# A two-layer macaron network on one core: tokens routed into a region per expert, group by group, and fp4 weights prepared inside the expert stage

## The reference

```
x = x + 0.5 * moe(norm(x))        # block 1
x = x + attention(norm(x))        # block 2, causal softmax, 16 heads
x = x + 0.5 * moe(norm(x))        # block 3, the same weights as block 1
x = x + 0.5 * fp4_ffn(norm(x))    # block 4
x = x + linear_attention(norm(x)) # block 5
x = x + 0.5 * fp4_ffn(norm(x))    # block 6, the same weights as block 4

moe(x):  e = argmax(x @ W_router)               # 4 experts, one per token
         h = gelu(x @ W1[e] + b1[e])            # 256 -> 1024
         return layer_norm(h @ Wo + bo + x) * gamma + beta
fp4_ffn: weights 704 x 256, 704 x 256 and 256 x 704, and the activations,
         quantised to fp4 and back in blocks of 16: scale = max|block| / 6,
         each value rounded to the grid 0, 0.5, 1, 1.5, 2, 3, 4, 6 times scale
```

## Time and profile before

| what | us |
|---|---|
| median of 3 runs (2399.11 to 2403.15) | 2401.53 |
| the profiled execution, time | 2399.69 |
| its span in the trace | 2397.8 |
| setup, up to the first routing stage | 17.3 |
| first routing stage: tiles, then the rest | 68.7, then 55.9 |
| first expert stage begins | 141.9 |
| second routing stage begins | 1062.4 |
| its tiles, then the rest | 73.4, then 64.9 |
| second expert stage begins | 1200.7 |
| busy over the span: TensorE, VectorE, ScalarE, GpSimd | 2047.2, 1446.0, 996.3, 970.0 |

### The profile page before, as it was taken

One profiled execution on the slowest core, in us unless ns is written; L12 is line 12 of the kernel. 1 busy time (PEld: TensorE's weight loads), 2 busy tenths in 40 slices (PEclk: granted clock), 3 DMA queues, 4 the chain that ended last, 5 costly groups with the idle time before them and its releaser, 6 DMA issues. The chain is left out here.

```text
span 2397.8 us, 43209 instructions
## 1 busy us (share of the span) xinstructions
PE 2047.2 (85%) x13577; PEld 1400.5 (58%) x13577; DVE 1446.0 (60%) x3844; ACT 996.3 (42%) x2303; POOL 970.0 (40%) x1249
## 2 busy tenths in 40 slices
PE   4359998696999999988289995899988999789996
PEld 3259897352444444437189994566665666456674
DVE  4313223667888888826623333889857676488883
ACT  1023332241666666653133332333325666534332
POOL 4422223750111111124612224666546666455652
PEclk9999999796999999999589997999999999999999
DMA  5145554346333344210255553000000000000002
GB/s 189 39 158 195 192 193 136 118 146 97 54 55 54 54 54 54 28 38 1 70 188 192 195 192 125 22 13 18 0 1 2 2 2 2 1 1 0 0 0 70
DMA packets 105499, 177.02 MB, mean 74 GB/s; under 512 B 14576, under 2 KB 70160, under 8 KB 105360
## 3 DMA queue, kind: packets, MB, share of 16 engines
q1 hardware_dynamic: 99216, 158.47, 24.0%
q0 software_dynamic: 6144, 16.79, 2.2%
HBM read 136.01 MB, written 38.93 MB: 73 GB/s over the span
## 5 line engine op out<-in xcount | busy, mean ns | idle before, releaser
L1024 DVE TENSOR_REDUCE a_part_max<-a_psS 128x1 f32<-128x512 f32 (+3 forms) x608 | 362.8, 655 | 76.2 <-PE a_psS L952 67.6
L1080 ACT ACTIVATE a_PT<-a_psE 128x512 f32<-128x512 f32 (+1 forms) x608 | 309.3, 583 | 189.1 <-PE a_psE L966 174.1
L518 PE MATMUL e_psH<-e_xsT,e_w 128*128 128x128 f32 x2240 | 266.7, 278 | 0.0
L518 PEld LDWEIGHTS e_psH<-e_xsT,e_w 128*128 128x128 f32 x2240 | 259.9, 194 | 0.6
L946 PE MATMUL a_psS<-a_sk,a_sq 96*128 96x512 bf16 (+3 forms) x768 | 234.3, 341 | 23.5 <-DMA a_sk<-qk_parts 19.6
L527 PE MATMUL e_psY<-wo_moe,e_gT 128*128 128x256 f32 x1120 | 253.0, 379 | 0.0
L927 POOL TENSOR_SCALAR_AFFINE_SELECT a_PT<-a_PT 128x512 f32<-128x512 f32 x128 | 81.5, 637 | 419.1 <-ACT a_PT L1080 419.1
L966 PE MATMUL a_psE<-a_sq,a_sk 98*128 98x512 bf16 (+3 forms) x768 | 224.6, 329 | 2.5 <-ACT a_PT L1080 1.4
L527 PEld LDWEIGHTS e_psY<-wo_moe,e_gT 128*128 128x128 f32 x1120 | 207.6, 190 | 25.4
L547 ACT ACTIVATE e_gT<-e_psH,e_bias 128x128 f32<-128x128 f32 x560 | 159.9, 369 | 138.6 <-PE e_psH L518 138.6
L567 DVE TENSOR_TENSOR e_y<-e_psY,e_xr 128x256 f32<-128x256 f32 x70 | 29.7, 425 | 308.1 <-PE e_psY L527 303.9
(11 more groups left out here) (269 smaller groups left out, 3869.1 us busy)
## 6 DMA issues: line engine op xcount, KB each, us to landing
e_w<-w_in SPq DMA_DIRECT2D x70, 1024.0 KB, 4.9
a_sq<-qk_parts SPq DMA_DIRECT2D x96, 128.0 KB, 4.4
a_sk<-qk_parts SPq DMA_DIRECT2D x96, 128.0 KB, 7.2
e_xs<-sorted_x SPq DMA_DIRECT2D x70, 128.0 KB, 2.1
e_xr<-sorted_x SPq DMA_DIRECT2D x70, 128.0 KB, 4.6
sorted_y<-e_yo SPq DMA_DIRECT2D x70, 128.0 KB
sorted_x<-zeros SPq DMA_DIRECT2D x1, 4480.0 KB, 18.8
X<-x_in SPq DMA_DIRECT2D x4, 1024.0 KB, 9.7
```

What stands on the lines that cost most here:

```text
L518: mm = pe.matmul(psH[p][:, n * P:(n + 1) * P], w1[p][:, k, n * P:(n + 1) * P], xsT[p][:, k, :], start=k == 0, stop=k == KD - 1)
L1024: dve.tensor_reduce(part_max[:, c, h0:h0 + heads, qt], psS[place % RING][:, 0:heads * n].rearrange("p (h k) -> p h k", h=heads), AX.X, ALU ...
L1080: act.activation(PT[kt % 2][:, h0:h0 + heads, q0:q0 + n], psE[e % RING][:, 0:heads * n].rearrange("p (h q) -> p h q", h=heads), ACT.Exp, s ...
```

## The change

1. **Regions.** Each expert has a region of 4224 rows in `sorted_x`, so a token's row is known from its rank within its expert, before the totals are. `choose` finds the expert for a group of four tiles, `count_up` ranks them with five matmuls, `put` makes the rows, and GpSimd scatters the group while later tiles are routed. At the end four more scatters write zeros behind each expert's last token. Tables say for each of the 35 tiles its expert and its row (`row_of`), and for each token its row in `sorted_y` (`result_row`), which stays dense.
2. **Normalisation** moves to ScalarE, straight into `XN`; the GpSimd copy goes. GpSimd takes one power for two tiles.
3. **Setup** keeps the first piece of x and the router's weights; the other loads are issued by SyncE in the first routing stage, x in pieces of four tiles.
4. **fp4 weights** are loaded in the second routing stage as before, but quantised in the second expert stage, in 18 pieces of 128 x 256, one per tile.
5. The hardware loops of routing and expert stages are written out (`loop=False`). Two constants that nothing used are dropped.

```diff
 TensorE, routing
-  [(1, project), (0, turn_y)] + [(5, router), (4, turn)]
+  [(1, project), (0, turn_y)] + [(J + 9, count_up, 4), (J + 4, router), (J + 3, turn)]    # J = 3 after attention, else 0
+            def count_up(t, p):
+                g = t // G
+                pe.wait_ge(choice, CHOICE * (g + 1))
...
+                mm = pe.matmul(psN[:, 0:GE], st.upper[:], oh[:].rearrange("p j e -> p (j e)"), start=True, stop=False,
+                               skip_group_check=True)
+                for j in range(G - 1):
+                    mm = pe.matmul(psN[:, (j + 1) * EXPERTS:GE].rearrange("p (j e) -> p j e", e=EXPERTS), st.ones[:],
...
+                if g > 0:
+                    mm = pe.matmul(psN[:, 0:GE].rearrange("p (j e) -> p j e", e=EXPERTS), st.ones[:],
...
+                mm.then_inc(ranked, 1)
 VectorE, routing
+            def choose(t, p):        # 7 chained instructions on 128 x 16
...
+            def put(t, p):           # 4 chained instructions on 128 x 16
...
+            pipeline(dve, TILES, ([(2, join)] if after_attention else []) +
+                     [(J, measure, 2), (J + 2, take_shift, 2), (J + 8, choose, 4), (J + 10, put, 4)], unroll=4, loop=False)
 ScalarE, routing
+            def norm(t, p):
+                i = p // 2
+                act.wait_ge(shifted, t // 2 + 1)
+                for j in (0, 1):
+                    act.activation(XN[:, t + j, :], st.X[:, t + j, :], ACT.Identity,
+                                   bias=shift[i][:, j:j + 1], scale=rstd[i][:, j:j + 1]).then_inc(normed, 1)
 GpSimd, routing
+            def scatter(t, p):
+                pool.wait_ge(placed, PLACED * (t // G + 1))
+                for j in range(G):
+                    pool.indirect_dma_start(st.sorted_x[:, :], bass.IndirectOffsetOnAxis(ap=st.slot[:, t + j:t + j + 1], axis=0),
+                                            XN[:, t + j, :], None).then_inc(scattered, 16)
+            pipeline(pool, TILES, [(J, root, 2), (J + 10, scatter, 4)], unroll=4, loop=False)
+            pool.wait_ge(padded, 2)
+            for e in range(EXPERTS):
+                pool.indirect_dma_start(st.sorted_x[:, :], bass.IndirectOffsetOnAxis(ap=pad_slot[:, e:e + 1], axis=0),
+                                        st.zeros[:], None).then_inc(scattered, 16)
 expert stage
+        def piece_of(t):
+            return t - 1 if fp4 and 1 <= t <= len(fp4.pieces) else None
-                sp.dma_start(xs[p][:], st.sorted_x[bass.ds(t * P, P), :]).then_inc(x_in[p], 16)
+                sp.dma_start(xs[p][:], st.sorted_x[bass.ds(row(sp, t), P), :]).then_inc(x_in[p], 16)
             def turn(t, p):                                                     # TensorE
                 pe.wait_ge(x_in[p], 8 * (t - p) + 16)
                 reuse(pe, evacuated, t)
+                if fp4:
+                    if piece_of(t - 2) is not None:
+                        pe.wait_ge(fp4.out, KD * (t - 2))
+                    if piece_of(t) is not None:
+                        fp4.turn(pe, piece_of(t), psT[p])
                 for k in range(KD):
                     mm = pe.transpose(psT[p][:, k * P:(k + 1) * P], xs[p][:, k * P:(k + 1) * P], st.ident[:])
-            pipeline(dve, SLOTS, [(0, take_bias), (2, finish), (3, norm)])
+            pipeline(dve, SLOTS, [(0, take_bias), (2, finish), (3, norm)] + ([(0, quantize_weights)] if fp4 else []),
+                     loop=False)
 class Fp4Weights
+    def turn(self, pe, n, ps):
+        pe.wait_ge(self.quant, self.STEPS * (n + 1))
+        src = self.source(n)
+        for k in range(KD):
+            mm = pe.transpose(ps[:, D + k * P:D + (k + 1) * P], src[:, k * P:(k + 1) * P], self.st.ident[:])
+        mm.then_inc(self.turned, 1)
```

More of the change, by code:

```diff
@@ L150, in _ @@
             x = st.x_in.rearrange("(t p) d -> p t d", p=P)
+            sp.dma_start(st.X[:, 0:4, :], x[:, 0:4, :]).then_inc(st.x_loaded[0], 16)
             sp.dma_start(st.w_router[:], st.router_in.rearrange("(k p) e -> p k e", p=P)).then_inc(st.router_loaded, 16)
[L152 to L161, removed]
         @block.gpsimd
@@ L279, in measure, with take_shift @@
                 take_moments_of_pair(dve, c, st.X, t, stats[i], moments[i], LN_EPS)
                 c.end()
-            def norm(t, p):
+            def take_shift(t, p):
                 i = p // 2
                 dve.wait_ge(rooted, t + 2)
[L285 to L289, removed]
@@ L310, in _ @@
[L310 to L317, removed]
@@ L342, in _ @@
[L342 to L345 removed]
+                if t >= 4:
+                    dve.wait_ge(normed, t - 2)
+                dve.scalar_tensor_tensor(out=shift[i][:], in0=moments[i][:, :, 0], scalar=-1.0, in1=rstd[i][:],
+                                         op0=ALU.mult, op1=ALU.mult).then_inc(shifted, 1)
@@ new lines, in _ @@
+            q.link(dve.scalar_tensor_tensor(out=rowf[:], in0=st.slot_f[:], scalar=float(P), in1=jump[:, 0, :],
+                                            op0=ALU.mult, op1=ALU.add))
+            for e in range(2, EXPERTS + 1):
+                if e < EXPERTS:
+                    q.done(dve.scalar_tensor_tensor(out=whichf[:], in0=st.slot_f[:], scalar=first[:, e:e + 1],
+                                                    in1=whichf[:], op0=ALU.is_ge, op1=ALU.add))
+                q.link(dve.tensor_tensor(rowf[:], rowf[:], jump[:, e - 1, :], ALU.add))
@@ L428, in _ @@
             if not after_attention:
                 pe.wait_ge(st.router_loaded, 16)
-            pipeline(pe, TILES, ([(1, project), (0, turn_y)] if after_attention else []) + [(5, router), (4, turn)],
-                     unroll=4, loop=not after_attention)
-            pe.wait_ge(sorting, 9)
-            oh = onehot[:].rearrange("p e t -> p (e t)")
-            pe.matmul(psN[:, 0:ET], st.upper[:], oh, start=True, stop=True)
-            pe.matmul(psN[:, ET:2 * ET], st.ones[:], oh, start=True, stop=True).then_inc(counted, 1)
@@ L437, in _ @@
-            if after_attention:
-                fp4.tensor(pe)
-            else:
+            pipeline(pe, TILES, ([(1, project), (0, turn_y)] if after_attention else []) +
+                     [(J + 9, count_up, 4), (J + 4, router), (J + 3, turn)], unroll=4, loop=False)
+            pe.wait_ge(placed, PLACED * NG)
+            pe.matmul(psN[:, GE:GE + EXPERTS], st.ones[:], before[NG % 2][:], start=True, stop=True).then_inc(counted, 1)
+            if not after_attention:
                 pe.wait_ge(st.weights_loaded, 16 * WEIGHT_LOADS)
@@ L529, in down_proj @@
                 mm.then_inc(down, 1)
-            pipeline(pe, SLOTS, [(0, turn), (1, up_proj), (2, down_proj)])
+            pipeline(pe, SLOTS, [(0, turn), (1, up_proj), (2, down_proj)], loop=False)
         @block.scalar
@@ L539, in evacuate @@
                                ACT.Copy).then_inc(evacuated, 1)
+                if fp4 and piece_of(t) is not None:
+                    fp4.put(act, piece_of(t), psT[p])
             def activate(t, p):
@@ L548, in activate @@
                 ins.then_inc(gelu, 1)
[L550 removed]
+            pipeline(act, SLOTS, [(0, evacuate), (1, activate)], loop=False)
         @block.vector
@@ L594, in scale @@
                 c.end()
-            pipeline(pool, SLOTS, [(0, root), (1, scale)])
+            pipeline(pool, SLOTS, [(0, root), (1, scale)], loop=False)
 class Gather:
@@ new lines, in clear, with quantize @@
+        dve.wait_ge(self.cleared, 1)
+        dve.wait_ge(self.loaded, 16 * 5)
+    def quantize(self, dve, n):
+        if n == 0:
+            self.clear(dve)
+        c = Chain(dve, self.quant, self.STEPS).at(n)
+        dve.wait_ge(self.quant, self.STEPS * n)
+        blocked = lambda a: a.rearrange("p (b e) -> p b e", e=BLOCK)
+        x, vv, mm = blocked(self.source(n)), blocked(self.v[:]), blocked(self.m[:])
+        back = quantize(dve, c, x, vv, mm, self.scale[:], self.inverse[:])
+        c.link(dve.tensor_tensor(vv, vv, mm, ALU.subtract))
+        c.done(dve.tensor_tensor(x, vv, back, ALU.mult))
+        c.end()
@@ L1918, in build @@
         st.w_down = sb("w_down", [P, KF, D])
-        run(route_phase, "r1_", True)
-        run(expert_phase, "e1_")
+        with ExitStack() as raw:
+            st.fp4 = Fp4Weights(nc, st, raw)
+            run(route_phase, "r1_", True)
+            run(expert_phase, "e1_", st.fp4)
         st.lin_w = sb("lin_w", [P, KD, 3 * D])
```

379 lines of the change are left out of this document (199 added, 180 removed).

## The result

The changed kernel takes 2455.68 us (median of 4 runs, 2454.3 to 2460.63); the kernel before, run beside it, takes 2400.34 (4 runs). The ratio is 1.0232 with a 95% interval of 1.022 to 1.0244: 2.3% slower. The forecast was 2488 with a range of 2440 to 2530. The profiled execution has a span of 2454.3 against 2397.8, so 56.5 us are to be placed.

What follows compares the result with a forecast made beforehand. TensorE was taken to bound the expert stage, a tile chain and GpSimd-only scatter tails the routing stages. 2399.7 - 35.6 (first routing) + 5 (first expert) - 30.2 (second routing) + 149 (second expert) = 2488 us; range 2440 to 2530.

Steps and rivals of the forecast that it cites:

- The stall in the second expert stage: Second expert stage: TensorE waits for each lap's quantize; 16 laps of 16.55 us against 7.49, +149 us with small terms.
- quantize hides: Rival, second expert stage: quantize runs in VectorE's idle time ahead of finish, routing gains stand; 2347 us, chance 0.06.
- The clock: Second expert stage: each pause drops TensorE to half clock for about 4 us, costing 2.0 us a lap (bounds 0 and 3).
- full clock: Rival, second expert stage: stalls as forecast, but TensorE's clock stays up; 2456 us, chance 0.16.
- Clock down all through: Rival, second expert stage: each of 16 stalled laps at half clock, costing 7.25 and not 2.0; 2572 us, chance 0.07.
- Start of routing: First routing stage: SyncE issues two small loads, so the setup barrier falls at about 5.8 instead of 17.3, -11.5 us.
- count_up: Routing stages: new TensorE matmuls cost 1.5 us a group, +10.5 in the first stage; +10 in the second.
- The tails: Both routing stages: last router to next stage shrinks to 20.7 us; -35.2 in the first, -44.2 in the second.
- routing gains halved: Rival, routing stages: GpSimd backlog and late X pieces cost +33; 2521 us, chance 0.07.
- exclusive lock: Routing scatters: if the port lock shared by VectorE and GpSimd made all issues 2.13 us long, the sum would be 2501.
- The register read: Expert stages: SyncE reads a register before token loads, 0.7 us each; +5 in the first, +3 in the second.
- The rest: Attention and the fp4 layers, outside routing and expert stages: not touched by the change, 0.

Runs made afterwards that it cites:

- x1: Changed kernel with VectorE doing the quantize first in its step instead of last: 2322.67 us, ratio 0.9676.
- x2: Changed kernel with VectorE's order kept, but TensorE takes each fp4 piece one lap later: 2322.83 us, ratio 0.9678.
- x5: Changed kernel with 48 unread identity transposes on TensorE ahead of each wait for a piece, from turn(3) on: 2421.59 us, ratio 1.0089.
- x8: Changed kernel with 2 instead of 5 matmuls in count_up, VectorE adding up the one-hot rows within the group first: 2439.6 us, ratio 1.0167.
- x6: Kernel before with the loops of both expert stages written out, nothing else: 2388.29 us, ratio 0.9956.
- x7: Changed kernel with the edits of x1 and x8 together: 2305.61 us, ratio 0.9608.
- x3: Changed kernel with the fp4 weights back at the end of the second routing stage, as before: 2353.7 us, ratio 0.9806.

## Why the prediction was right

The mechanism was the predicted one, at its predicted place, and the time lies 32 us under the forecast. That is inside the range, but below the 2465 to 2515 given for the mechanism alone.

- **The stall in the second expert stage** (+149, measured +134.3). The condition "It decides if quantize(s) ends before down(s-2) does" was put to the test by x1 and x2, and each took out 133 us, all of the slowdown and more. That is *quantize hides* made true, at 2323 where 2347 was given; 18.7 of the 24 us between them are the routing stages and the first expert stage, which came out better than forecast here too. There are 16 stalled laps and two free pieces, as counted. A lap was priced at 16.55; it takes 15.95. The term that was mis-sized is the idle: 7.0 assumed, 6.53 measured, within the bounds of 6.1 to 7.5. That is 7.5 us over 16 laps. I had let six VectorE instructions wait for GpSimd to end, from L1171 on. L1171 did not: it ran beside GpSimd and took 0.54, against 0.42 in the first stalled lap (1143.02), where GpSimd was idle. L1172 may have waited: it took 0.70 instead of 0.29, and ended 0.15 or 0.16 us behind GpSimd's L652 in each of the 15 laps behind that one. One instruction (0.42 and a gap of 0.04) is what the 7.0 had too much. Of the other 7, no run separates the parts: a lap of x5 less its wait, 13.76 less 6.45, is 7.31, where I had counted 7.25 and 0.3 (4 us over 16 laps), and the free laps gained from the written-out loops, for which I had counted nothing.
- **The clock** (2.0 a lap): 2.1 by x5 on the mean. The "about 4 us after work began" of the forecast came from one pause; here it was 2.9, 4.8 or 5.8, and that their mean of 4.5 lies so near is partly luck. This is what tells *full clock* from the forecast. That rival's number, 2456, is the measured time to the microsecond, and its mechanism is still wrong. With the clock up the changed kernel would have taken 2421.6. The two numbers meet because the routing stages gained 10.4 us more, the first expert stage 8.3 more and the second lost 14.7 less than forecast. A total alone can't confirm a mechanism. The Trainium skill (TensorE: Matmul & The Clock Gate, "HAM oscillation — how this bites in real kernels") describes such a loop, whose waits are for transfers; here the same comes from a wait for another engine, at 6.53 us of pause and 2.1 us of loss on the mean.
- ***Clock down all through*** fell: from 1183.70 on the lap runs at 1.00, and no lap looked at stays at 0.50 for more than 5.8 us of its work.
- **Start of routing** (-11.5): -12.5. First routing begins at 4.85, not 17.3.
- **count_up** (1.5 a group): 1.25, the 3.26 less 2.01 above. In the second routing stage I added 10 for it and 4 for two more steps of the pipeline. Its tiles grew from 73.4 to 80.7, by 7.3 in all, so half of that 14 was not there. x8 confirms the kind and the size.
- **The tails** (20.7 each): 21.1 in the first stage, 20.9 in the second, whose last router matmul ends at 1099.63. The scatters spread over the tiles as foreseen, and *routing gains halved* fell: 64 scatters took 0.98 us each on the mean, the longest seen 1.22, so GpSimd never fell behind. The sum by an exclusive lock did not come. The 2501 given for it holds the 13 us of one routing stage only; for both it would have been 2514. The Trainium skill (SBUF — State Buffer, "Who interferes with whom") says that a VectorE instruction with two inputs in SBUF contends with a GpSimd instruction that reads SBUF. The trace agrees in the expert stage, where L1171 took 0.54, and L1253, of the same shape and alone, 0.42. For L1171 those 0.12 us are far less than a whole GpSimd instruction (L652, 0.79). For L1172, by its 0.41 us and its end just behind L652, a wait for the whole of it is not ruled out.
- **The register read** (+5 in the first expert stage): the step's own size was right, 4.6 us by the comparison with x6. The sign of the stage came out wrong (-3.3) because I had valued the written-out loops at a mere bound, "which is in the bound 0", and x6 shows them at 7.7 and 6.3 us a stage from first load to 35th (7.0 and 5.9 over the whole stages).
- **The rest** (+2.4, forecast 0): between the first transpose of the first fp4 layer and the last store, where the code is the same, seven of the profiled kernels (all but x2, x5 and x7) took 881.4 to 884.3 us. The changed kernel took 883.3 and the kernel before 881.7, so 1.6 of it is within what these kernels differ by where their code is the same. What the remaining 0.8 is stays open.

## What to carry to other kernels

Work that another engine will wait for doesn't belong at the end of a step behind an instruction that waits for that same engine. Put it first in the step, or let the consumer ask a lap later; either was worth 5% here and cost little: from the first token load to the 35th the second expert stage takes 248.7 us in x1, against 246.3 in x3, which has no quantize in it. Ask of every added instruction what stands ahead of it in its engine's order, and not whether the engine has time. And price a regular pause of TensorE at more than its length: here 6.5 us of waiting cost 2.1 more on the mean.

## What the runs showed of the hardware that was not expected

- The same pause does not cost the same each time. Behind a constant 6.53 us TensorE ran at 1.2 GHz for about 2.9, 4.8 or 5.8 us, in turn, and lost 1.3, 2.2 or 2.7 us by it (the changed kernel's laps of 15.2, 16.1 and 16.6 us less x5's 13.77 and the 0.08 by which x5 waits less).
- The clock column of a view can say 1.00 where rows show 1.2 GHz: the router's four loads took 0.93 us throughout the first routing stage, as at 0.50 in the second.
- The expert stages' hardware loops cost 14.0 us between the first and the 35th token load of the two stages (x6, 249.7 to 242.0 and 248.4 to 242.2), though TensorE was nearly full there; 9.9 of it reached the kernel's time.
- One read of a register from a table ahead of a load moves that load by 0.72 us on SyncE (1.09 behind the store against 0.37).
- Two small matmuls with their four weight loads (1.1 us), set into an idle 0.87 us of TensorE, cost next to nothing: in x8 the tile with count_up takes 2.02 us, as the others do (2.01 in the earlier trace rows).
